# A gated RWKV mix and a quantised FFN in one kernel: second norm's statistics in three parts, 1/sqrt by ScalarE with a Newton step on Pool, norms halved between ScalarE and Pool

## The reference

```python
x = x + tanh(g_xattn) * birwkv(r=layernorm(x), k=ctx, v=ctx, w, u)   # sigmoid(r) * (sums of e^k v) / (sums of e^k)
x = x + tanh(g_ffn) * ffn(layernorm(x), ...)

def layernorm(x):                       # over the 256 channels, eps 1e-5
    return (x - mean(x)) / sqrt(var(x) + eps)

def ffn(x, ...):                        # fake quantisation to 8 bits
    xq = act_quant(x, clip_x)           # scale from max |x| over the WHOLE tensor
    h = act_quant(silu(xq @ wq_gate.T) * (xq @ wq_up.T), clip_down)
    return h @ wq_down.T
```

## Time and profile before

| | us |
|---|---|
| median of 3 runs | 221.23 (219.24 to 221.35) |
| the profiled execution | 221.53 |
| its span, first to last instruction | 220.1 |
| mean granted clock of TensorE | 0.882 of full speed |
| busy: PE, DVE, ACT, POOL | 172.1, 170.5, 156.0, 138.5 |

### The profile page before, as it was taken

One profiled execution on the slowest core, in us unless ns is written; L12 is line 12 of the kernel. 1 busy time (PEld: TensorE's weight loads), 2 busy tenths in 40 slices (PEclk: granted clock), 3 DMA queues, 4 the chain that ended last, 5 costly groups with the idle time before them and its releaser, 6 DMA issues.

```text
span 220.1 us, 3345 instructions
## 1 busy us (share of the span) xinstructions
PE 172.1 (78%) x1098; PEld 124.4 (57%) x1098; DVE 170.5 (77%) x344; ACT 156.0 (71%) x234; POOL 138.5 (63%) x157
## 2 busy tenths in 40 slices
PE   4499968989898999971076649959999943999960
PEld 4456528979898999960065533414343412776620
DVE  0769493648558689986699679496899998999992
ACT  3459698555995996987489965747998953899400
POOL 3455223559699799865788609984577670029991
PEclk9969996999999999998566755997999995599996
DMA  3999999999998995200000000000000000004468
GB/s 102 328 374 348 348 314 291 271 294 298 291 317 204 279 248 159 83 0 1 0 0 0 0 0 3 1 0 0 0 3 0 0 1 0 0 3 141 149 201 275
DMA packets 43328, 29.31 MB, mean 133 GB/s; under 512 B 2224, under 2 KB 43056, under 8 KB 43312
## 3 DMA queue, kind: packets, MB, share of 16 engines
q1 hardware_dynamic: 43168, 28.84, 45.8%
q10 hardware_dynamic: 144, 0.26, 0.3%
HBM read 24.65 MB, written 4.46 MB: 132 GB/s over the span
## 4 chain that ended last, share of the span: by engine, by line
PE 43%; ACT 14%; DVE 12%; DMA 9%; POOL 7%; issue 7%; SPq 6%; DVEq 1%; POOLq 0%; ACTq 0%
PE ps L1011 12%; PE ps L978 11%; PE ps L882 7%; PE ps L898 7%; DMA hidden<-lag_w 6%; PE ps L922 4%; DMA hidden<-in_ctx 3%; ACT hidden L499 3%; ACT z_t L506 2%; SPq L271 2%; PE ps L929 2%; ACT hidden L570 2%; POOL z_t L433 2%; DVE h_peaks L817 1%; SPq L278 1%
## 5 line engine op out<-in xcount | busy, mean ns | idle before, releaser
L898 PE MATMUL ps<-hidden 128*128 128x128 f32 (+1 forms) x512 | 60.5, 280 | 5.6 <-DVE hidden L645 2.5
L898 PEld LDWEIGHTS ps<-hidden 128*128 128x128 f32 x512 | 59.5, 196 | 7.1 <-issue 3.3
L397 POOL TENSOR_TENSOR x_all<-x_all,silu_out 128x512 f32<-128x512 f32 x16 | 24.4, 1537 | 8.1 <-DVE silu_out L707 8.0
L817 DVE TENSOR_REDUCE h_peaks<-hidden (+2 forms) x24 | 26.0, 1123 | 3.6 <-POOL hidden L441 3.2
L698 DVE SCALAR_TENSOR_TENSOR h_space<-z_t,ps 128x256 f32<-128x256 f32 x32 | 19.1, 600 | 10.9 <-PE ps L898 10.8
L1011 PE MATMUL ps<-wdT,z_t 128*128 128x256 bf16 (+1 forms) x192 | 26.0, 293 | 1.9 <-ACT z_t L629 1.9
L922 PE MATMUL ps<-ident,hidden 128*128 128x128 f32 x64 | 13.1, 374 | 15.9 <-POOL hidden L421 11.4
L629 ACT ACTIVATE z_t<-h_space 128x1024 bf16<-128x1024 int8 (+3 forms) x12 | 20.1, 1754 | 6.8 <-DVE h_space L845 6.8
L1011 PEld LDWEIGHTS ps<-wdT,z_t 128*128 128x128 bf16 (+1 forms) x192 | 17.6, 104 | 10.3 <-issue 4.8
L615 ACT ACTIVATE silu_out<-ps,mix_scale 128x1024 f32<-128x1024 f32 (+1 forms) x18 | 18.4, 1020 | 5.5 <-PE ps L978 3.2
L922 PEld LDWEIGHTS ps<-ident,hidden 128*128 128x128 f32 x64 | 10.8, 197 | 18.0 <-ACT hidden L499 17.3
(11 more groups left out here) (101 smaller groups left out, 340.8 us busy)
## 6 DMA issues: line engine op xcount, KB each, us to landing
hidden<-lag_w SPq DMA_DIRECT2D x26, 512.0 KB, 7.3
x_all<-in_x SPq DMA_DIRECT2D x8, 512.0 KB, 8.8
hidden<-in_ctx SPq DMA_DIRECT2D x8, 512.0 KB, 9.0
out<-x_all SPq DMA_DIRECT2D x16, 256.0 KB, 2.3
xq<-in_L_ffn_w_down SPq DMA_DIRECT2D x1, 704.0 KB, 5.9
xq<-in_L_ffn_w_gate SPq DMA_DIRECT2D x1, 640.0 KB, 7.3
h_space<-in_L_ffn_w_up SPq DMA_DIRECT2D x1, 640.0 KB, 6.0
lag_w<-up_out ACTq DMA_DIRECT2D x1, 255.0 KB, 7.4
```

The costliest lines, as they stand in the source:

```text
L397: nc.gpsimd.tensor_tensor(xs, xs, mixed[:, m % 2, :, :].rearrange("p c b -> p b c"), ALU.add).then_inc(s["x1_done"], 1)
L817: nc.vector.tensor_reduce(h_peaks[:, bass.ds(KA * b + k, 1)], hidden[:, bass.ds(b * HB + k * BT, cols)], AX.X, ALU.max, apply_absolute_val ...
L898: last = nc.tensor.matmul(ps[:, j % BANKS, c * 2 * SEQS:end * 2 * SEQS], lag_tile(j)[:, c, :], ekp[:, (j * CK + c) * 2 * SEQS:(j * CK + en ...
```

## The change

The statistics of the second norm are taken in three parts instead of two: channels 0 to 127 after m = 9, 10 and 11 of the loop (11, 11 and 10 sequences), channels 128 to 191 after m = 13 and 14 (16 sequences each), channels 192 to 255 after the loop. 1/sqrt(var + eps) comes from ScalarE as Exp(-0.5 Ln(var + eps)) with one Newton step on Pool, for sets of one, three and four groups at once, in place of Pool's `pow` for each group. Each group's norm is split two and two between ScalarE and Pool. VectorE takes all late statistics before all peaks. The table load with Tanh moves from before the norms to behind the eviction of group 6. Scratch for the sets lies in `up_out`.

```diff
@@ -198,12 +198,18 @@
         rs1 = sb("rs1", [P, GS])
         nr1 = sb("nr1", [P, SEQS])
         mr1 = sb("mr1", [P, SEQS])
-        bn2 = sb("bn2", [P, SEQS, 2, 6])
+
+        PARTS = [0, 8, 12, PAIRS]
+        SETS = [(0, 1), (1, 4), (4, GROUPS)]
+        bn2 = sb("bn2", [P, SEQS, len(PARTS) - 1, 6])
         mv2 = sb("mv2", [P, SEQS, 2])
-        ve2 = sb("ve2", [P, GS])
         rs2 = sb("rs2", [P, SEQS])
-        nr2 = sb("nr2", [P, SEQS])
         mr2 = sb("mr2", [P, SEQS])
+        ve2, ln2, raw2, sq2 = [up_out[:, 512 + i * SEQS:512 + (i + 1) * SEQS] for i in range(4)]
+
+        def set_of(g):
+            return [i for i, (first, end) in enumerate(SETS) if first <= g < end][0]
+
         consts = sb("consts", [P, 3, GS])
 
         s = {n: sem(n) for n in (
...
@@ -358,17 +364,26 @@
                 nc.gpsimd.tensor_tensor(nr, rs1[:, :], consts[:, 2, :], ALU.mult)
                 nc.gpsimd.tensor_tensor(mr, rs1[:, :], mean, ALU.mult).then_inc(s["sc1_done"], 1)
 
-            def rstd2(g):
-                pool.wait_ge(s["mv2_done"], g + 1)
-                mean, var = mv2[:, g * GS:(g + 1) * GS, 0], mv2[:, g * GS:(g + 1) * GS, 1]
-                rs, nr, mr = [t[:, g * GS:(g + 1) * GS] for t in (rs2, nr2, mr2)]
-                nc.gpsimd.tensor_tensor(ve2[:, :], var, consts[:, 1, :], ALU.add).then_inc(s["ve2_done"], 1)
-                pool.wait_ge(s["ve2_done"], g + 1)
-                nc.gpsimd.tensor_tensor(rs, ve2[:, :], consts[:, 0, :], ALU.pow).then_inc(s["rs2_done"], 1)
-                pool.wait_ge(s["rs2_done"], 2 * g + 1)
-                nc.gpsimd.tensor_tensor(nr, rs, consts[:, 2, :], ALU.mult).then_inc(s["rs2_done"], 1)
-                pool.wait_ge(s["rs2_done"], 2 * g + 2)
-                nc.gpsimd.tensor_tensor(mr, nr, mean, ALU.mult).then_inc(s["sc2_done"], 1)
+            def rstd2(i):
+
+                first, end = SETS[i]
+                rows_ = slice(first * GS, end * GS)
+                mean, var = mv2[:, rows_, 0], mv2[:, rows_, 1]
+                raw, ve, sq, rs, mr = [tile[:, rows_] for tile in (raw2, ve2, sq2, rs2, mr2)]
+                pool.wait_ge(s["mv2_done"], end)
+                nc.gpsimd.tensor_scalar(ve, var, EPS, 1.0, ALU.add, ALU.mult).then_inc(s["ve2_done"], 1)
+                pool.wait_ge(s["raw2_done"], i + 1)
+                nc.gpsimd.tensor_tensor(sq, raw, raw, ALU.mult).then_inc(s["ve2_done"], 1)
+                pool.wait_ge(s["ve2_done"], 2 * i + 2)
+                nc.gpsimd.tensor_tensor(sq, sq, ve, ALU.mult).then_inc(s["rs2_done"], 1)
+                pool.wait_ge(s["rs2_done"], 4 * i + 1)
+                nc.gpsimd.tensor_scalar(sq, sq, -0.5, 1.5, ALU.mult, ALU.add).then_inc(s["rs2_done"], 1)
+                pool.wait_ge(s["rs2_done"], 4 * i + 2)
+                nc.gpsimd.tensor_tensor(rs, raw, sq, ALU.mult).then_inc(s["rs2_done"], 1)
+                pool.wait_ge(s["rs2_done"], 4 * i + 3)
+                nc.gpsimd.tensor_tensor(mr, rs, mean, ALU.mult).then_inc(s["rs2_done"], 1)
+                pool.wait_ge(s["rs2_done"], 4 * i + 4)
+                nc.gpsimd.tensor_scalar(mr, mr, -1.0, 0.0, ALU.mult, ALU.add).then_inc(s["sc2_done"], 1)
 
             def own_weights(i):
 
@@ -414,19 +429,18 @@
                     add_own(MADE.index(j))
                     if j != MADE[-1]:
                         own_weights(MADE.index(j) + 1)
-            def normalise_last(g):
-
-                n = g * GS + GS - 1
-                pool.wait_ge(s["sc2_done"], g + 1)
-                nc.gpsimd.tensor_scalar(z_all[:, n * C:(n + 1) * C], x_all[:, n * C:(n + 1) * C], rs2[:, n:n + 1],
-                                        mr2[:, n:n + 1], ALU.mult, ALU.add).then_inc(s["z_last"], 1)
-
-            rstd2(0)
-            for g in range(GROUPS):
-                if g + 1 < GROUPS:
-                    rstd2(g + 1)
-                normalise_last(g)
-
+            def normalise_late(g):
+
+                pool.wait_ge(s["sc2_done"], set_of(g) + 1)
+                for n in range(g * GS + GS // 2, (g + 1) * GS):
+                    last = nc.gpsimd.tensor_scalar(z_all[:, n * C:(n + 1) * C], x_all[:, n * C:(n + 1) * C], rs2[:, n:n + 1],
+                                                   mr2[:, n:n + 1], ALU.mult, ALU.add)
+                last.then_inc(s["z_last"], 1)
+
+            for i, (first, end) in enumerate(SETS):
+                rstd2(i)
+                for g in range(first, end):
+                    normalise_late(g)
 
             for n in range(2, GROUPS):
                 pool.wait_ge(s["x8_done"], n + 1)
@@ -490,11 +504,20 @@
                 wait(act, s["mix_done"], 2 * m - 2)
                 nc.scalar.activation(rden[:, m % 2, :], lnd, ACT.Exp, scale=-1.0).then_inc(s["rden_done"], 1)
 
+            def rstd2(i):
+
+                first, end = SETS[i]
+                rows_ = slice(first * GS, end * GS)
+                act.wait_ge(s["mv2_done"], end)
+                nc.scalar.activation(ln2[:, rows_], mv2[:, rows_, 1], ACT.Ln, bias=consts[:, 1, 0:1]).then_inc(s["ln2_done"], 1)
+                act.wait_ge(s["ln2_done"], i + 1)
+                nc.scalar.activation(raw2[:, rows_], ln2[:, rows_], ACT.Exp, scale=-0.5).then_inc(s["raw2_done"], 1)
+
             def normalise(g):
 
-                act.wait_ge(s["sc2_done"], g + 1)
+                act.wait_ge(s["sc2_done"], set_of(g) + 1)
                 xs = seqs(x_all[:, :], g * GS, GS)
-                for i in range(GS - 1):
+                for i in range(GS // 2):
                     n = g * GS + i
                     last = nc.scalar.activation(z_all[:, n * C:(n + 1) * C], xs[:, i, :], ACT.Identity,
                                                 scale=rs2[:, n:n + 1], bias=mr2[:, n:n + 1])
@@ -584,11 +607,13 @@
                 if m == 12:
                     exp_clips()
             keep_weights(2)
+            for i, (first, end) in enumerate(SETS):
+                rstd2(i)
+                for g in range(first, end):
+                    normalise(g)
+                    if g > 0:
+                        keep_z(g - 1)
             tanh_ffn()
-            normalise(0)
-            for g in range(1, GROUPS):
-                normalise(g)
-                keep_z(g - 1)
 
             def cast_first():
 
@@ -667,20 +692,21 @@
                     last = nc.vector.bn_aggr(mv1[:, g * GS + i, :], bn1[:, i, :])
                 last.then_inc(s["mv1_done"], 1)
 
-            def stats2(n, h):
-                return nc.vector.bn_stats(bn2[:, n, h, :], x_all[:, n * C + h * P:n * C + (h + 1) * P])
-
-            def early_stats(first, n):
-
-                dve.wait_ge(s["x1_done"], PAIRS // 2)
+            def stats2(part, n):
+                first, end = PARTS[part] * 2 * CK, PARTS[part + 1] * 2 * CK
+                return nc.vector.bn_stats(bn2[:, n, part, :], x_all[:, n * C + first:n * C + end])
+
+            def early_stats(part, first, n):
+
+                dve.wait_ge(s["x1_done"], PARTS[part + 1])
                 for i in range(first, first + n):
-                    stats2(i, 0)
+                    stats2(part, i)
 
             def late_stats(g):
 
                 dve.wait_ge(s["x1_done"], PAIRS)
                 for i in range(GS):
-                    last = stats2(g * GS + i, 1)
+                    last = stats2(len(PARTS) - 2, g * GS + i)
                 last.then_inc(s["bn2_done"], 1)
                 dve.wait_ge(s["bn2_done"], g + 1)
                 for i in range(GS):
@@ -743,7 +769,6 @@
             nc.vector.tensor_scalar(lag_abs, lag_abs, -1.0, 0.0, ALU.add, ALU.max).then_inc(s["lag_abs_done"], 1)
             denominator(0)
             denominator(1)
-            done = 0
             for m in range(PAIRS):
                 if m + 1 < PAIRS:
                     denominator(2 * m + 2)
@@ -761,16 +786,13 @@
                     down_diagonals()
                 if m == 13:
                     sigmoid_clips()
-                if m > 9:
-                    n = min(6, SEQS - done)
-                    early_stats(done, n)
-                    done += n
-            assert done == SEQS
+                if 9 <= m < 12:
+                    early_stats(0, 11 * (m - 9), min(11, SEQS - 11 * (m - 9)))
+                if 13 <= m < 15:
+                    early_stats(1, SEQS // 2 * (m - 13), SEQS // 2)
             for g in range(GROUPS):
-                if g >= 3:
-                    peak_z(g - 3)
                 late_stats(g)
-            for g in range(GROUPS - 3, GROUPS):
+            for g in range(GROUPS):
                 peak_z(g)
 
             def global_peak(tile, prefix, quotient, scale, inverse):
```

(2 more changed lines are left out.)

## The result

The change makes the kernel slower: 225.66 us median against 220.24, and 1.0203 as a ratio of paired runs, with a 95% interval of 1.0134 to 1.0273. That is +4.5 us, with an interval of 3.0 to 6.0; the prediction said 225.0, by +3.7 on the profiled execution. The profile after is of the longest of the four executions, 227.44 us; the other three took 223.99 to 225.73.

The account below looks back on a forecast made before the run. Bound: nearly full engines until 97.5 us, then a chain of waits from 104.2 to 130.0. Profiled 221.53 + 4.0 (loop) - 0.3 (second norm) = 225.2, some 225.0 at the median; 8-in-10 range 221.8 to 227.0.

Parts of the forecast that it names:

- Early statistics: Mixing loop: regrouped and added VectorE statistics delay its end by 4.0 us; 3.6 to 5.5 by the small statistic's price.
- Denominator 22: Loop, after m = 9: 11 statistics queued ahead of it on VectorE make it slide 2.1 us, to 86.9.
- mix 20: Loop: VectorE step that now ends at 87.9 instead of 85.8, so TensorE's chunk 26 waits 1.8 us.
- Chunk 30: Loop, TensorE: waits on Pool's additions behind ScalarE's delayed lag weights; 94.39 becomes 97.5, 3.1 us late.
- another 0.9: Loop, after m = 14: 16 small statistics instead of six stand between mixes 29 and 30, 2.1 for 1.17 us.
- Second norm: Stage after the loop: batched scale and halved norms gain 0.3 us, between 0.2 and about 1.1 by transpose speed.
- The holes of 1.8 and 1.9: Second norm: ScalarE idles ahead of the norms of groups 1 and 4, waiting for Pool's scale.
- four gains: Second norm: four gains of half a microsecond, paid back by two idle holes of ScalarE; 0.3 us taken.
- Table load: Behind the eviction of group 6: 1.28 us, then Tanh 0.20; hidden ahead of the first cast by 0.4.
- A: Loop absorbs the extra statistics, only 0.9 at m = 14 stays: about 222.0, 219 with a quicker tail; chance 0.12.
- D: Second norm: Ln and Exp bring table reloads, five of 1.28 us, giving 231; chance 0.04.
- C: TensorE's clock falls in the loop's new waits; last two chunks +1.8 us each, partly on the path: 227; chance 0.10.
- B: Denser tail lifts TensorE's clock for gate and up: up to 3 us back, 222 or so; chance 0.10.

Follow-up runs that it names:

- the bursts alone: Changed kernel with two parts only: 11, 11 and 10 statistics of 128 channels after m = 9, 10 and 11, none later in the loop; 222.07 us.
- The two runs on the parts: Changed kernel with the statistics' old parts and places, ratio 1.002; kernel before with only the three parts and their new places, ratio 1.0172.
- the small ones added: Changed kernel with the 128-channel statistics back at their old places and the 64-channel ones kept after m = 13 and 14; 223.04 us.

## Why the prediction was right

The result lies 0.7 us above the predicted 225.0 and inside its range, and the steps can be held against the rows one by one.

**Early statistics.** A statistic of 64 channels was priced at 0.13 us and measured at 0.127. Eleven of 128 channels were put at 2.1 and took 2.14 (88.12 to 90.26). Denominator 22 slides by that much behind the diagonals, and TensorE waits 1.69 for mix 20, where 1.8 was forecast. Chunk 30 was to be 3.1 late: it starts 12.69 us after the diagonals' end, 9.63 before, so 3.06. After m = 14 another 0.9 was forecast: the bursts alone give +2.99 and the whole +3.93, so 0.94. The loop in all: +4.0 predicted, +3.93 measured. One estimate in the prediction counts too much: at 0.142 for a small statistic the sum was to grow by 0.4, 0.2 for each burst. The 0.2 after m = 13 would have been covered, since VectorE idled 0.33 us ahead of denominator 31 (106.14).

**Second norm.** The gain was predicted at 0.3 and measured at 0.51. The scale of a set was to take 2.25 from the statistics, and the norm of group 0 to come 3.4 after X; it came at 3.50 (114.98). The 0.1 is in the statistics: four `bn_aggr` over three parts take 0.52 us where four over two took 0.42, and the prediction left them at the old price. The holes of 1.8 and 1.9 measured 1.79 and 1.83, the transposes of group 0 came at 4.83 where 4.6 was forecast, and Ln with a pointer took 0.30 for 0.29. Pool's small operations took 0.20 with 0.08 between, as predicted, and 0.22 for 16 columns. Up to the transposes of group 7 the gain is 0.2, as summed; the other 0.3 comes behind them, where those transposes took 1.09 us and before 1.84. The two runs on the parts share the 0.51 out otherwise than "four gains" and "two holes" suggest: the shorter statistics alone give 0.40, the new norm alone 0.04.

**Table load.** It took 1.28 us with 0.20 for Tanh, behind the eviction of group 6, as predicted (134.81). The last eviction ended at 137.22, while the first cast, at 137.43, waited 0.21 us for VectorE's quantised block: the load stayed hidden, by 0.2 where 0.4 was expected. The 0.4 had been held against the cast's old time, without the 0.3 that the norm was to gain. ScalarE's Tanh began 1.29 us after the load's start here too. The Trainium skill (ScalarE: Activation LUTs, what a table load costs) gives 2.66 us for a switch; no run here shows that.

**What stays.** D to Q makes +3.43, the time outside the span another 0.44, for which the prediction has no term: 3.9 together. The paired runs say +4.5 with an interval that holds it. The remainder, 0.6, is less than what the two outer lengths differ by from one execution to the next, so it can't be put down to the change. That the forecast came within 0.7 us of the median is therefore in part luck; that the loop came within 0.1 is not.

The rivals: A (the loop absorbs it) and D (reloads) are out, one table load is in the trace after 100 us. C (the clock falls in the loop's waits) did not occur: the two chunks behind the wait of 1.69 us took 3.75, the chunk behind the wait of 1.73 took 2.00 as before, and the granted clock was 1.00 in both. B came about in part and paid nothing: the ten microseconds from Q ran at 0.83 in both profiles after (last section) and at 0.63 before, and yet Q to the end was 90.3 us in one of them, as long as before. VectorE was busy 9.9 of these 10 us in all three profiles, which is the likely reason.

## What to carry to other kernels

Work put into an engine's idle time costs by what stands behind it in that engine's queue, not by its total: the same 32 statistics in the loop cost 3.0 us when grouped in front of a denominator that two engines were waiting for. When a per-group chain is batched into sets, the set's latency becomes a hole unless the first step of the next set is issued while the current set still has work: moving two small activations up by two evictions and a norm was worth 2.7 us in the stage. And where one part relieves an engine and another loads it, the two should be tried together as well as alone: halving the norms and batching the scale lost 2.7 and 2.8 us alone and broke even together.

## What the runs showed of the hardware

Two executions of the same changed kernel differ in the stretch before the diagonals by 4.4 us, the ten profiles of this case by as much (83.5 to 88.1). In the one that ended it at 88.1, TensorE waited 2.28 and 2.13 us for lag weights, up to 47.5 and 58.8; in the other 1.59 and 0.74, up to 46.1 and 56.0, and in the kernel before 1.05 and 0.69, up to 47.2 and 57.0. The program of the first two is the same; why the transfers landed later stays open, and these waits make up about half of the 4.4.

The last stage has two lengths, 88.6 to 88.8 and 90.2 to 90.3 us, without a change in the program: the changed kernel showed both. Its windows of ten microseconds from Q (length; PE, PEld, DVE, ACT, POOL busy; granted clock, DMA share, GB/s), first profile:

```profile
136.64:146.64 10.00, 7.25 (x27) 2.83 (x28) 9.94 (x10) 7.88 (x8) 7.58 (x6) 0.83 0.01 2
...
146.64:156.64 10.00, 6.66 (x33) 2.69 (x35) 6.95 (x7) 5.73 (x7) 7.65 (x4) 1.00 0.00 0
```

and the same kernel again:

```profile
132.22:142.22 10.00, 7.75 (x28) 3.02 (x28) 9.94 (x10) 7.30 (x8) 7.58 (x6) 0.83 0.01 2
...
142.22:152.22 10.00, 6.86 (x28) 2.35 (x27) 6.95 (x7) 5.07 (x6) 7.64 (x4) 0.84 0.00 0
```

The granted clock is 1.00 against 0.84 in the second window, with the same 0.83 in the first. The ten profiles agree with that: the three with the shorter length (the first profile of the change, the bursts alone and the small ones added) show 1.00 in the second window, the other seven 0.84 to 0.89, and the clock of the first, 0.63 to 0.83, does not go with the length. Whether the clock sets the length or follows from it is not shown. The stretch from Q to the peak of the hidden tensor was 51.7 us in the first profile, 53.2 in the second and 53.1 in the kernel before.
